# Attention in groups of three token tiles behind accumulating gathers, and gate sums fetched by DMA

## The chip, the cores and the metric

One core of a Trainium2 chip runs the whole kernel as one program. The metric is device time in microseconds (us). Three runs of the kernel before took 1563.63, 1563.95 and 1555.30 us, median 1563.63.

## The reference, cut to what matters

```
h = tok(x)                                    # patches of 16 frames, layer norm, matmul, layer norm
h = h + power_attention(layernorm(h))         # 8 heads x 2 queries, gates
h = h + experts(layernorm(h))                 # top 4 of 16 experts, and a shared one
h = h + rope_softmax_attention(layernorm(h))  # 16 heads, 4 key heads
h = h + bitlinear_ffn(layernorm(h))

# power attention, per head
logG = cumsum(log_sigmoid(6.906768 + x @ Wg))
a = (q k^T / sqrt(d))**2 * exp(logG[t] - logG[s]), causal;  y = (a @ v) / sum(a)

# experts
acc + cw[:, None] * (silu(x @ wg.T) * (x @ wu.T)) @ wd.T      # cw is 0 outside a token's top 4
```

There are 64 sequences of 23 tokens, so T = 1472 tokens, in NT = 12 tiles of 128 rows. All sums are f32; a product is split in two f16 halves and made as three matmuls (`split3`, L852 to L854).

## The kernel before

Five instruction streams (SP for most transfers, POOL for indirect and other transfers and small arithmetic, ACT, PE, DVE) run side by side and meet at semaphores. There is no scheduler: the order on every engine is the order in the text.

**First attention.** A loop over 8 heads and, in it, over 4 chunks c of 16 sequences (CW = 368 tokens, as four blocks of AT = 92). For each chunk PE projects q, q and k (`head_project`, 12 matmuls each), then v (48 matmuls), makes the squared scores' products (L950), the output projection of the chunk before (`out_proj`), the weighted sum (L967), and turns the result (L983). The gate exponent logG[t] - logG[s] needs, in each of 92 partitions, the sum of one head's gates along the row. Before, that row is made anew for each chunk: DVE multiplies the log gates by a triangle (L1447, tile `Dg`), PE multiplies by a matrix of ones (L935), ACT copies it from PSUM (L635, tile `gt`), and DVE subtracts logG and adds the mask (L1450, L1452). At the end of a head ACT and DVE split the next head's weights in halves (`unit_a_hi` L550, `unit_a_lo` L1295), and in chunks 1 and 3 one expert's weights (`expert_hi` L627, `expert_lo` L1295).

Ahead of the first head, PE computes the gate logits (`gate_logits`), DVE and ACT their log sigmoid, and PE sums it (L904) before it projects anything.

**Experts.** A token's rows go to expert tiles of 128 slots; results are kept in DRAM (`yslot`, L480). The shared expert's tiles 6 to 11 come last. Then 48 indirect transfers (12 tiles x 4, `collect`, L484) fetch each token's four results to a scratch tile, three tiles deep, and DVE adds them up and into the row h (`returned`, L1698 to L1701). Statistics of the rows (`total_stats`, L1313), a root on POOL (L446) and shifts (L1327) follow for tiles 0 to 7 and then for 8 to 11.

**Second attention.** ACT normalizes 12 tiles (L560), PE turns them (L847), ACT and DVE split them (L565, L1332). Then the chunks c = 0 to 3 of 368 tokens: PE makes six projections (`project`: j = 0 to 3 q, 4 k, 5 v, the last at L1161), ACT moves them (`moved`, L743, L738), DVE shuffles (L1743), POOL multiplies by cosine and sine (`cosine`, L516, L517), DVE adds (`rotated`, L1753, L1754), PE makes 16 x 4 small score products (`scores`, L1177), DVE masks and centres (L1761, L1764, L1765), ACT exponentiates (L747), DVE divides (`weights`, L1771, L1772, L1777), PE turns (`turn`, L1186) and multiplies by V (`weighted`, L1199), and ACT and DVE split the result (L760, L1784). The output projection (`out_rows`), the last norm and the feed-forward layer follow.

PE's order there is scores(c), project(c + 1, 0 to 5), turn(c), weighted(c), scores(c + 1). All 12 tiles are turned before scores(0).

## Time and profile before

| | |
|---|---|
| median of three runs | 1563.63 us |
| profiled execution | 1547.85 us, span 1545.9 us |
| mean granted TensorE clock | 0.915 |
| busy: PE, DVE, ACT, POOL | 1316.9, 937.2, 644.0, 283.0 us |
| start to 143 us | tokens and first norms |
| 143 to about 707 us | first attention, 8 heads |
| about 707 to 1124 us | routing and experts |
| 1124 to 1190 us | 48 gathers |
| 1190 to 1341 us | second attention |
| 1341 us to the end | output projection, feed-forward |

Times in the rows are counted from the span's start. A busy time that is larger than the distance to the next start means pipelined work: for matmuls the distance between starts is what one costs. "idle before <- X" names what the engine waited for. The clock is a share of the full 2.4 GHz, so 0.50 is 1.2 GHz.

### The profile page before, as it was taken

How to read it: one execution, taken by the hardware profiler on the slowest of the kernel's cores; microseconds unless marked ns; L12 is line 12 of the kernel's file. 1: busy time of each engine (PE TensorE's matmuls, PEld its weight loads, DVE VectorE, ACT ScalarE, POOL GpSimd, SP SyncE). 2: the span in 40 equal slices, each digit the busy share in tenths (PEclk: the TensorE clock that was granted, in tenths of full speed). 3: DMA queues.
4: the chain of work that ended last, by engine and by line, in shares of the span. 5: the costliest groups of instructions: out<-in, count | busy, mean ns of one | idle time of the engine just before them, and what ended most of it. 6: DMA issues, size and time to landing. Idle time of an engine off the chain costs nothing.

```text
span 1545.9 us, 30851 instructions
## 1 busy us (share of the span) xinstructions
PE 1316.9 (85%) x10735; PEld 837.6 (54%) x10736; DVE 937.2 (61%) x1940; ACT 644.0 (42%) x1098; POOL 283.0 (18%) x342
## 2 busy tenths in 40 slices
PE   6887999999999999996759999999950788668997
PEld 3445767677776777774424444444520566424443
DVE  5775456556665555658663555554376455588886
ACT  3445434444444444542314444444420433126664
POOL 2443000000000000000012233233276334020000
PEclk9986999999999999996779999999985778689999
DMA  5222142423334342421315767874265000000000
GB/s 177 69 102 69 56 170 116 163 109 135 133 132 170 136 163 82 163 83 75 132 62 181 258 240 256 283 241 162 91 193 168 2 2 3 1 1 8 21 20 31
DMA packets 40254, 179.87 MB, mean 116 GB/s; under 512 B 8512, under 2 KB 9024, under 8 KB 32384
## 3 DMA queue, kind: packets, MB, share of 16 engines
q0 software_dynamic: 18208, 95.41, 17.4%
q1 hardware_dynamic: 18528, 71.03, 13.0%
q10 hardware_dynamic: 3456, 12.58, 2.4%
q8 instruction: 41, 0.67, 0.2%
q14 instruction: 21, 0.17, 0.0%
HBM read 131.32 MB, written 47.69 MB: 116 GB/s over the span
## 4 chain that ended last, share of the span: by engine, by line
PE 56%; DVE 18%; issue 13%; POOL 6%; ACT 5%; DVEq 1%; DMA 1%; ACTq 0%; POOLq 0%; SPq 0%
PE ps L852 14%; PE ps L853 13%; PE ps L854 13%; POOL wide L484 3%; PE ps L967 3%; PE ps L950 3%; PE ps L1177 2%; DVE ff L1870 2%; DVE amf L1877 1%; PE ps L935 1%; PE ps L983 1%; DVE wa_lo L1295 1%; POOL rt_out L446 1%; PE ps L1046 1%; PE ps L1248 1%
## 5 line engine op out<-in xcount | busy, mean ns | idle before, releaser
L852 PE MATMUL ps<-nT_hi,wa_hi 128*128 128x368 f16 x448 | 146.4, 327 | 15.9 <-DVE wa_lo L1295 15.9
L853 PE MATMUL ps<-nT_lo,wa_hi 128*128 128x368 f16 x448 | 146.0, 326 | 0.0
L854 PE MATMUL ps<-nT_hi,wa_lo 128*128 128x368 f16 x448 | 145.6, 325 | 0.0
L476 POOL DMA_INDIRECT xg<-xrow,idx x61 | 61.1, 1001 | 277.1 <-PE ps L1046 101.7
L1629 DVE SCALAR_TENSOR_TENSOR nrm<-ps,xg,nrm 128x256 f32<-128x256 f32 x61 | 29.5, 484 | 133.5 <-ACT nrm L694 107.6
L852 PE MATMUL ps<-wa_hi,nT_hi 128*92 128x128 f16 (+1 forms) x560 | 108.8, 238 | 0.0
L853 PE MATMUL ps<-wa_lo,nT_hi 128*92 128x128 f16 (+1 forms) x560 | 107.6, 236 | 0.0
L854 PE MATMUL ps<-wa_hi,nT_lo 128*92 128x128 f16 (+1 forms) x560 | 107.6, 236 | 0.0
L852 PE MATMUL ps<-wide,xT 128*128 x244 | 93.4, 383 | 12.3 <-issue 6.3
L663 ACT ACTIVATE yT_hi<-ps 128x368 f16<-128x368 f32 x64 | 27.2, 474 | 164.0 <-PE ps L983 164.0
L471 POOL DMA_DIRECT2D wsp<-we_sp x16 | 8.6, 537 | 468.7 <-DVE we_sp L1295 468.7
L1432 DVE SCALAR_TENSOR_TENSOR wide<-ps,wide 128x368 f32<-128x368 f32 x128 | 69.1, 540 | 41.0 <-PE ps L854 41.0
L853 PE MATMUL ps<-wide,xT 128*128 x244 | 93.2, 382 | 0.0
L854 PE MATMUL ps<-wide,xT 128*128 x244 | 93.0, 381 | 0.0
L1248 PE MATMUL ps<-qw,qT 128*128 128x512 bf16 x384 | 89.1, 387 | 2.7 <-DVE ff L1870 2.6
L852 PE MATMUL ps<-yT_hi,wb_hi 128*128 128x368 f16 x256 | 82.6, 323 | 1.2 <-DVE yT_lo L1479 1.2
L853 PE MATMUL ps<-yT_lo,wb_hi 128*128 128x368 f16 x256 | 82.6, 323 | 0.0
L854 PE MATMUL ps<-yT_hi,wb_lo 128*128 128x368 f16 x256 | 82.6, 323 | 0.0
L622 ACT ACTIVATE qk<-ps 128x368 f32<-128x368 f32 x96 | 45.2, 478 | 89.1 <-PE ps L854 89.0
L1457 DVE TENSOR_TENSOR a<-sq,E 92x368 f32<-92x368 f32 x64 | 31.7, 534 | 82.3 <-ACT sq L651 82.3
L852 PEld LDWEIGHTS ps<-wa_hi,nT_hi 128*92 128x92 f16 (+1 forms) x560 | 67.4, 120 | 22.3 <-ACT qk L622 17.2
L685 ACT ACTIVATE xT<-ps 128x1024 f16<-128x1024 f16 x61 | 62.3, 1024 | 28.9 <-PE ps L1046 21.2
(307 smaller groups left out, 3403.9 us busy)
## 6 DMA issues: line engine op xcount, KB each, us to landing
we_st<-in_we POOLq DMA_DIRECT2D x16, 1536.0 KB, 6.9
wsp<-we_sp POOLq DMA_DIRECT2D x16, 1536.0 KB, 5.4
wide<-wsp SPq DMA_DIRECT2D x16, 1536.0 KB, 7.4
yslot<-yt POOLq DMA_DIRECT2D x61, 256.0 KB, 4.3
wq_st<-in_ffq SPq DMA_DIRECT2D x24, 512.0 KB, 4.5
wq_st<-in_ffq ACTq DMA_DIRECT2D x24, 512.0 KB, 3.9
wide<-in_wa SPq DMA_DIRECT2D x10, 1024.0 KB, 4.8
xt<-in_x SPq DMA_DIRECT2D x12, 512.0 KB, 3.5
```

The source lines that it names most:

```text
L476: pool.indirect_dma_start(Q["xg"][:, g % 4, :].bitcast(U32), None, xrow, bass.IndirectOffsetOnAxis(ap=idx[:, g:g + 1], axis=0)).then_inc(x ...
L484: pool.indirect_dma_start(h1[:, 4 * (k % 3) + j, :], None, yslot, bass.IndirectOffsetOnAxis(ap=slot[:, k, j:j + 1], axis=0)).then_inc(xg_i ...
L622: nc.scalar.activation(B["qk"][:, j, :], ps[:, (5 * c + j) % 2, 0:CW], ACT.Copy, scale=1.0 / WS).then_inc(b_ev, 1)
L685: nc.scalar.activation(Q["xT"][:, p].rearrange("p a b -> p (a b)"), ps[:, p, :].bitcast(F16), ACT.Copy).then_inc(m_xe, 1)
L852: nc.tensor.matmul(dst, lhs[0], rhs[0], start=start, stop=False)
L853: nc.tensor.matmul(dst, lhs[0], rhs[1], start=False, stop=False)
L854: return nc.tensor.matmul(dst, lhs[1], rhs[0], start=False, stop=stop)
L950: ins = nc.tensor.matmul(ps[0:AT, 2 + j, a * REP * AT:(a + 1) * REP * AT], B["qk"][:, 2, tok], B["qk"][:, 0:2, tok], start=True, stop=True)
L967: ins = nc.tensor.matmul(ps[0:AT, 4 + 2 * j + a, r * (DH + 1):(r + 1) * (DH + 1)], B["a"][0:AT, j, a, r, :], B["v1"][0:AT, 2 * j + a, :], ...
L1248: ins = nc.tensor.matmul(ps[:, 2 * (f % 2) + q, :], Gm["qT"][:, b, ds(k * P, P)], qw[:, q, b * FF + f * 512:b * FF + (f + 1) * 512], start ...
L1432: V.scalar_tensor_tensor(acc, ps[:, 6 + blk % 2, 0:CW], 1.0 / (WS * AS), acc, ALU.mult, ALU.add).then_inc(b_acc, 1)
L1457: V.tensor_tensor(B["a"][0:AT, j], B["sq"][0:AT, j], B["E"][0:AT, 2 * j:2 * j + 2].unsqueeze(2).broadcast_to([AT, 2, REP, AT]), ALU.mult). ...
```

## The change

(1) The gate sums are made once. PE forms them for all heads with the heads on partitions (a second small matmul beside L904's), DVE copies them (`lgt`), SP writes them to DRAM (`lgd`) and, for each head, fetches the row of one head broadcast to 92 partitions (`gr`, 92 x 1472 f32, 541.7 KB). L1447, L935 and L635 go. The first two projections now stand ahead of the gate sums on PE. At the end of a head the next head's weights are split ahead of the expert's.

(2) The 48 gathers add into the rows h themselves (`compute_op=ALU.add`). The four of one tile run one behind the other: each waits for the one before. DVE's four additions of a tile go. Those of tiles 0 to 5 are issued in rounds of six; those of tiles 6 to 11 in rounds of three, between POOL's other work.

(3) Statistics, roots, normalization and turning of the rows run in groups of three tiles, two groups ahead of or between the chunks of the second attention, which on PE now runs as project(c, 2 to 5), turn(c - 1), scores(c), weighted(c - 1), with the first two projections of a chunk ahead of it. DVE makes the sine products of chunk 0 and of j = 4. Scores wait for the copy out of PSUM (`f_cp`), no longer for the split result of the chunk just before.

```diff
-        h1 = flat.rearrange("p (k d) -> p k d", d=D)
...
+        lgd = nc.dram_tensor("lgd", (HEADS, T), F32, kind="Internal").ap()
...
+sp.wait_ge(g_lg, 2)
+sp.dma_start(lgd.rearrange("h (a p) -> (h a) p", p=AT), B["lgt"][:, :]).then_inc(init_out, 16)
+sp.wait_ge(init_out, 32)
+sp.dma_start(B["gr"][0:AT], lgd[0:1, :].broadcast_to([AT, T])).then_inc(gr_in, 16)
+with sp.Fori(0, HEADS - 1) as i:
...
     unit_b(i + 1)
+    sp.wait_ge(b_gr, i + 1)
+    sp.dma_start(B["gr"][0:AT], lgd[ds(i + 1, 1), :].broadcast_to([AT, T])).then_inc(gr_in, 16)
...
-def collect(k):
-    for j in range(TOPK):
-        pool.indirect_dma_start(h1[:, 4 * (k % 3) + j, :], None, yslot,
-                                bass.IndirectOffsetOnAxis(ap=slot[:, k, j:j + 1], axis=0)).then_inc(xg_in[k % 3], 16)
...
+def share(k, j):
+    if j or k >= 6:
+        pool.wait_ge(sh_in[k % 6], SHARES[k % 6] + 64 * (k // 6) + 16 * j)
+    pool.indirect_dma_start(h[:, k, :], None, yslot, bass.IndirectOffsetOnAxis(ap=slot[:, k, j:j + 1], axis=0),
+                            compute_op=ALU.add).then_inc(sh_in[k % 6], 16)
+def shares(g, j):
+    for k in range(GT * g, GT * g + GT):
+        share(k, j)
...
-for k in range(NT):
-    if k >= 3:
-        pool.wait_ge(c_h, ready(NT + k - 3))
-    collect(k)
...
-for n, x in enumerate((slice(0, EARLY), slice(EARLY, NT))):
-    root(rc_ask, 2 + n, rt_in[:, x], rt_out[:, x], rc_done)
...
+def turned_root(g):
+    x = slice(GT * g, GT * g + GT)
+    root(rc_ask, 2 + g, rt_in[:, x], rt_out[:, x], rc_done)
...
-    nc.gpsimd.tensor_tensor(Fm["qs"][:, j, :], Fm["qs"][:, j, :], sinT[:], ALU.mult).then_inc(f_cos, 1)
...
+    if c and j < 4:
+        nc.gpsimd.tensor_tensor(Fm["qs"][:, j, :], Fm["qs"][:, j, :], sinT[:], ALU.mult).then_inc(f_cos, 1)
...
+for j in range(TOPK):
+    shares(0, j)
+    shares(1, j)
+pool.wait_ge(m_y, VT)
+shares(2, 0)
+turned_root(0)
+nc.gpsimd.memset(Fm["qp"][:, :, :, SL:], 0.0).then_inc(f_pad, 1)
+shares(3, 0)
+turned_root(1)
+cosine(0, 0)
+shares(2, 1)
+cosine(0, 1)
+cosine(0, 2)
+shares(2, 2)
+cosine(0, 3)
+cosine(0, 4)
+shares(2, 3)
+pool.wait_ge(wa_lo, UNITS + 1)
+nc.gpsimd.memset(st_a[:], 0.0).then_inc(f_pad, 1)
+shares(3, 1)
+for j in range(5):
+    cosine(1, j)
+shares(3, 2)
+turned_root(2)
+shares(3, 3)
+turned_root(3)
+for c in range(2, CH):
     for j in range(5):
         cosine(c, j)
-    if c == 0:
-        nc.gpsimd.memset(Fm["qp"][:, :, :, SL:], 0.0).then_inc(f_pad, 1)
-        pool.wait_ge(wa_lo, UNITS + 1)
-        nc.gpsimd.memset(st_a[:], 0.0).then_inc(f_pad, 1)
...
-        act.wait_ge(b_pj, 5 * g + 4)
-        nc.scalar.activation(B["gt"][0:AT].rearrange("p a b -> p (a b)"),
-                             ps[0:AT, (5 * c + 3) % 2, 0:CW], ACT.Copy).then_inc(b_ev, 1)
...
+        if c == CH - 1:
+            unit_a_hi(i + 1, b_pj, 4 * CH * (i + 1))
         if c in (1, 3):
             expert_hi(2 * i + c // 2)
-        if c == CH - 1:
-            unit_a_hi(i + 1, b_pj, 5 * CH * (i + 1))
...
+def normed(k):
+    if k % GT == 0:
+        act.wait_ge(ln_sh, 3 + k // GT)
+    ln_norm(2, k, k % 2)
...
+normed(0)
+normed(1)
+high(0)
+normed(2)
+high(1)
+high(2)
+moved(0, 0)
+moved(0, 1)
 for c in range(CH):
-    if c + 1 < CH:
-        for j in range(2):
-            moved(c + 1, j)
-    exponential(c)
-    if c + 1 < CH:
-        for j in range(2, 6):
-            moved(c + 1, j)
-    weights_turned(c)
-    y_high(c)
+    k = GT * (c + 1)
+    if c % 2 == 0:
+        normed(k)
+        normed(k + 1)
+    moved(c, 2)
+    if c % 2 == 0:
+        high(k)
+        normed(k + 2)
+    moved(c, 3)
+    if c % 2 == 0:
+        high(k + 1)
+    moved(c, 4)
+    if c % 2 == 0:
+        high(k + 2)
+    moved(c, 5)
+    if c == 0:
+        act.wait_ge(wa_in, 16 * (UNITS + 1))
+        nc.scalar.activation(wo[0][:].rearrange("p a b -> p (a b)"), st_a[:], ACT.Copy, scale=WS).then_inc(wa_hi, 1)
+    else:
+        weights_turned(c - 1)
+    if c == 1:
+        normed(k)
+        normed(k + 1)
+        exponential(c)
+        y_high(c - 1)
+        high(k)
+        normed(k + 2)
+        high(k + 1)
+        high(k + 2)
+        moved(c + 1, 0)
+        moved(c + 1, 1)
+    else:
+        if c + 1 < CH:
+            moved(c + 1, 0)
+            moved(c + 1, 1)
+        exponential(c)
+        if c:
+            y_high(c - 1)
+weights_turned(CH - 1)
+y_high(CH - 1)
 def f_square(k, p, half):
...
-pe.wait_ge(g_lg, 1)
-nc.tensor.matmul(ps[0:AT, 7, 0:16 * HEADS], tri[0:AT, :], B["lg"][0:AT].rearrange("p a b -> p (a b)"),
-                 start=True, stop=True).then_inc(g_cum, 1)
...
-        pe.wait_ge(b_ev, free(5 * g + 3))
-        pe.wait_ge(b_D, g + 1)
-        nc.tensor.matmul(ps[0:AT, (5 * c + 3) % 2, 0:CW], ones[0:AT, 0:AT], B["Dg"][0:AT].rearrange("p a b -> p (a b)"),
-                         start=True, stop=True).then_inc(b_pj, 1)
-        pe.wait_ge(b_ev, free(5 * g + 4))
+        pe.wait_ge(b_ev, free(4 * g + 3))
...
 for j in range(2):
     head_project(0, 0, j)
+pe.wait_ge(g_lg, 1)
+nc.tensor.matmul(ps[0:AT, 7, 0:16 * HEADS], tri[0:AT, :], B["lg"][0:AT].rearrange("p a b -> p (a b)"),
+                 start=True, stop=True)
+nc.tensor.matmul(ps[:, 6, 0:AT], B["lg"][0:AT].rearrange("p a b -> p (a b)"), tri[0:AT, :],
+                 start=True, stop=True).then_inc(g_cum, 1)
 with pe.Fori(0, HEADS - 1) as i:
     head(i, False)
 head(HEADS - 1, True)
...
+    if j == 0:
+        pe.wait_ge(ln_lo, ready(2 * NT + GT * c + GT - 1))
...
-    if c:
-        pe.wait_ge(f_lo, 4 * c)
+    if c == 1:
+        pe.wait_ge(f_cp, 1)
+    if c > 1:
+        pe.wait_ge(f_lo, 4 * (c - 1))
...
     pe.wait_ge(f_s, c + 1)
+    pe.wait_ge(ln_lo, ready(2 * NT + min(NT, GT * (c + (3 if c % 2 else 2))) - 1))
...
     pe.wait_ge(f_ev, 6 * c + 7)
+    if c + 1 < CH:
+        pe.wait_ge(f_cp, c + 2)
+    else:
+        pe.wait_ge(f_lo, 4 * c)
...
-for k in range(NT):
-    ln_turn(2 * NT + k, k % 2, 2 + k % 4, 2 * NT + k - 1)
-    if k == 6:
-        pe.wait_ge(wa_lo, UNITS)
-    if k in (6, 8, 10):
...
+def row_turn_l1(k):
...
+for k in range(GT):
+    row_turn_l1(k)
+pe.wait_ge(wa_lo, UNITS)
...
+project(0, 0)
+project(0, 1)
 for c in range(CH):
+    k = GT * (c + 1)
+    for j in range(2, 6):
+        project(c, j)
+        if c % 2 == 0 and j < 5:
+            row_turn_l1(k + j - 2)
+    if c:
+        turn(c - 1)
+    if c == 0:
+        project(c + 1, 0)
+        project(c + 1, 1)
     scores(c)
-    if c + 1 < CH:
-        for j in range(6):
-            project(c + 1, j)
-    turn(c)
-    weighted(c)
+    if c == 1:
+        weighted(c - 1)
+        for j in range(GT):
+            row_turn_l1(k + j)
+    if 0 < c < CH - 1:
+        project(c + 1, 0)
+        project(c + 1, 1)
+    if c > 1:
+        weighted(c - 1)
+turn(CH - 1)
+weighted(CH - 1)
...
     pe.wait_ge(w_h, free(k))
+    pe.wait_ge(f_lo, 4 * ((min(T, P * k + P) - 1) // CW) + 4)
...
 dve.wait_ge(g_cum, 1)
+V.tensor_copy(B["lgt"][:], ps[:, 6, 0:AT]).then_inc(g_lg, 1)
...
-        V.tensor_tensor(B["Dg"][0:AT], B["lgh"][0:AT, 4 * c:4 * c + 4].unsqueeze(2).broadcast_to([AT, 4, AT]),
-                        tri[0:AT].unsqueeze(1).broadcast_to([AT, 4, AT]), ALU.mult).then_inc(b_D, 1)
-        dve.wait_ge(b_ev, ready(5 * g + 3))
-        order(V.tensor_tensor(B["gt"][0:AT], B["gt"][0:AT],
+        if c == 0:
+            dve.wait_ge(gr_in, 16 * (i + 1))
+            dve.sem_inc(passed, 1)
+        order(V.tensor_tensor(B["gt"][0:AT], B["gr"][0:AT, c * CW:(c + 1) * CW].rearrange("p (a t) -> p a t", a=4),
                               B["LGh"][0:AT, 4 * c:4 * c + 4].unsqueeze(2).broadcast_to([AT, 4, AT]), ALU.subtract))
+        if c == CH - 1:
+            dve.sem_inc(b_gr, 1)
         V.tensor_tensor(B["gt"][0:AT], B["gt"][0:AT], mask[0:AT].unsqueeze(1).broadcast_to([AT, 4, AT]),
...
+        if c == CH - 1:
+            unit_a_lo(i + 1)
         if c % 2:
             expert_lo(2 * i + c // 2, 0)
-        if c == CH - 1:
-            unit_a_lo(i + 1)
...
-def returned(k):
-    dve.wait_ge(xg_in[k % 3], SLOTS_IN[k % 3] + 64 * (k // 3 + 1))
-    dve.sem_inc(passed, 1)
-    y = [h1[:, 4 * (k % 3) + j, :] for j in range(TOPK)]
-    V.tensor_tensor(y[0], y[0], y[1], ALU.add)
-    order(V.tensor_tensor(y[2], y[2], y[3], ALU.add))
-    order(V.tensor_tensor(row(k), row(k), y[0], ALU.add))
-    V.tensor_tensor(row(k), row(k), y[2], ALU.add).then_inc(c_h, 1)
...
-    dve.wait_ge(c_h, ready(NT + k))
+    dve.wait_ge(sh_in[k % 6], SHARES[k % 6] + 64 * (k // 6 + 1))
...
+def group_stats(g):
+    for k in range(GT * g, GT * g + GT):
+        total_stats(k)
+    deviations(2, GT * g, GT * g + GT, rc_ask)
...
+def group_shift(g):
+    shifts(2 + g, GT * g, GT * g + GT, rc_done)
...
+group_stats(0)
+group_shift(0)
+group_stats(1)
...
+    if c == 0 or j == 4:
+        dve.wait_ge(f_sh, 5 * c + j + 1)
+        dve.sem_inc(passed, 1)
+        V.tensor_tensor(Fm["qs"][:, j, :], Fm["qs"][:, j, :], sinT[:], ALU.mult).then_inc(f_cos, 1)
...
     dve.wait_ge(f_sc, c + 1)
...
+    V.tensor_tensor(S.rearrange("p (g h) s -> p g h s", g=G4),
+                    ps[:, 2:6, 0:CW].rearrange("p g (h s) -> p g h s", s=SL),
+                    mask1[:].unsqueeze(1).unsqueeze(1).broadcast_to([P, G4, 16, SL]), ALU.add).then_inc(f_cp, 1)
+    dve.wait_ge(f_cp, c + 1)
...
+for k in range(GT):
+    low(k)
+group_shift(1)
 for c in range(CH):
+    k = GT * (c + 1)
+    rotate(c, 0)
+    rotate(c, 1)
+    if c:
+        weights(c - 1)
+    for j in range(2, 5):
+        if c % 2 == 0:
+            low(k + j - 2)
+        rotate(c, j)
+    rotated(c)
+    if c == 0:
+        dve.wait_ge(wa_hi, UNITS + 1)
+        split_lo(wo[1][:].rearrange("p a b -> p (a b)"), st_a[:], wo[0][:].rearrange("p a b -> p (a b)"), wa_lo)
+    if c == 1:
+        group_stats(2)
+        group_shift(2)
     centred(c)
-    if c + 1 < CH:
-        for j in range(2):
-            rotate(c + 1, j)
-    weights(c)
-    if c + 1 < CH:
-        for j in range(2, 5):
-            rotate(c + 1, j)
-        rotated(c + 1)
-    y_low(c)
+    if c:
+        y_low(c - 1)
+    if c == 1:
+        for j in range(GT):
+            low(k + j)
+        group_stats(3)
+        group_shift(3)
+weights(CH - 1)
+y_low(CH - 1)
```

## Rows read from the trace of the kernel before

**Rows 1.** Windows: us, busy of PE, PEld, DVE, ACT, POOL (instructions), PE clock, DMA share, GB/s
```profile
283.40:351.80 68.40, 66.09 (x568) 49.76 (x568) 40.55 (x80) 30.00 (x51) 2.15 (x4) 1.00 0.37 138
...
1124.30:1190.30 66.00, 18.48 (x99) 8.57 (x97) 46.17 (x80) 9.18 (x16) 51.62 (x49) 0.68 0.69 201
1190.30:1229.00 38.70, 22.51 (x304) 16.21 (x304) 20.40 (x39) 19.50 (x31) 14.36 (x14) 0.72 0.03 11
1229.00:1259.60 30.60, 25.53 (x528) 19.25 (x528) 15.46 (x22) 9.36 (x16) 9.33 (x10) 0.78 0.01 3
...
1317.20:1340.60 23.40, 12.65 (x273) 11.54 (x274) 9.00 (x6) 3.82 (x5) 0.00 (x0) 0.53 0.01 1
```

**Rows 2.** Timeline of PE, end of a head and next chunk: start, busy, line, shape, idle before
```profile
285.68 0.33 PE L852 MATMUL ps<-nT_hi,wa_hi 128*128 128x368 f16 x1 [2.28 <-DVE wa_lo L1295]
...
287.56 0.80 PE L983 MATMUL ps<-ident,yn 92*128 92x92 f32 x8
288.19 0.32 PE L852 MATMUL ps<-nT_hi,wa_hi 128*128 128x368 f16 x1
...
295.67 0.79 PE L935 MATMUL ps<-Dg,ones 92*92 92x368 f32 x2
296.40 0.26 PE L852 MATMUL ps<-wa_hi,nT_hi 128*92 128x128 f16 x1
```

**Rows 3.** Timeline of DVE at the same head boundary
```profile
283.26 2.29 DVE L1295 SCALAR_TENSOR_TENSOR wa_lo<-wide,wa_hi 128x2048 f16<-128x2048 f32 x1
...
286.85 0.69 DVE L1473 TENSOR_TENSOR yn<-ps,rn 92x512 f32<-92x512 f32 x1
```

**Rows 4.** Timeline of PE at the start of the first attention
```profile
151.30 0.73 PE L904 MATMUL ps<-lg,tri 92*92 92x128 f32 x2 [6.13 <-DVE lg L1418]
...
165.52 0.72 PE L967 MATMUL ps<-v,a 92*92 92x129 f32 x5
```

**Rows 5.** DMA issues: tile, queue, kind, count, KB each, median us to landing
```profile
xt<-in_x SPq DMA_DIRECT2D x12, 512.0 KB, 3.5
...
tb<-in_tb SPq DMA_DIRECT2D x1, 256.0 KB, 9.2
...
xrow<-cwt SPq DMA_DIRECT2D x1, 96.0 KB, 2.6
```

**Rows 6.** The gathers, L484: durations on POOL in ns, and to landing
```profile
L484 POOL DMA_INDIRECT wide<-yslot,slot x48: 942/948/2623, 1124.3 to 1189.2; - x48
...
DMA to landing us min/median/max: 3.3/3.7/7.3
```

**Rows 7.** Timeline of PE in the second attention
```profile
1197.39 1.97 PE L847 MATMUL ps<-ident,nrm 128*128 128x128 f32 x8 [52.36 <-ACT nrm L560]
...
1228.94 7.04 PE L1177 MATMUL ps<-kr,qp 32*128 32x23 f32 x128 [6.87 <-DVE qp L1754]
1235.91 0.49 PE L852 MATMUL ps<-nT_hi,wa_hi 128*128 128x368 f16 x1
1239.57 0.51 PE L852 MATMUL ps<-nT_hi,wa_hi 128*128 128x368 f16 x1
1241.80 0.32 PE L852 MATMUL ps<-nT_hi,wa_hi 128*128 128x368 f16 x1
1243.67 0.32 PE L852 MATMUL ps<-nT_hi,wa_hi 128*128 128x368 f16 x1
```

**Rows 8.** Timelines of DVE, ACT and POOL in the second attention
```profile
1236.05 1.69 DVE L1761 TENSOR_TENSOR wide<-ps,mask 128x1472 f32<-128x1472 f32 x1 [7.16 <-PE ps L1177]
...
1247.56 1.69 DVE L1777 TENSOR_TENSOR wide<-wide,rd 128x1472 f32<-128x1472 f32 x1
...
1243.79 1.43 ACT L747 ACTIVATE wide<-wide 128x1472 f32<-128x1472 f32 x1
...
1241.76 0.97 POOL L516 TENSOR_TENSOR qraw<-qraw,cosT 128x368 f32<-128x368 f32 x1 [13.06 <-DVE qs L1743]
```

**Rows 9.** Timeline of PE, last chunk of the second attention
```profile
1334.97 3.83 PE L1186 MATMUL ps<-ident,wide 128*128 128x128 f32 x16 [10.74 <-DVE wide L1777]
```

More of the change, by code:

```diff
@@ L390, in _ @@
                 unit_b(i + 1)
+                sp.wait_ge(b_gr, i + 1)
+                sp.dma_start(B["gr"][0:AT], lgd[ds(i + 1, 1), :].broadcast_to([AT, T])).then_inc(gr_in, 16)
+            sp.wait_ge(q_abs, 3 * HEADS - 2)
+            for m in range(3):
+                sp.dma_start(wq_st[:, m, :], t["ffq"][m, HEADS - 1]).then_inc(q_in, 16)
+            sp.wait_ge(wa_lo, HEADS)
+            unit_a(HEADS)
+            sp.wait_ge(wb_lo, HEADS)
+            unit_b(HEADS)
             for k in range(NT):
@@ L760, in y_high @@
                     nc.scalar.activation(cols, ps[:, 2 + j, 0:CW].rearrange("p (w a t) -> p a w t", w=4, a=J4), ACT.Copy).then_inc(f_hi, 1)
-            for k in range(NT + 1):
-                if k in (0, EARLY):
-                    act.wait_ge(ln_sh, 3 + k // EARLY)
-                if k < NT:
-                    ln_norm(2, k, k % 2)
-                if k:
-                    ln_high(2 * NT + k - 1, k - 1, 2 + (k - 1) % 4)
-                if k in (8, 10, 12):
-                    moved(0, (k - 8) // 2)
@@ L918, in head_project @@
             def head_project(g, c, j):
-                pe.wait_ge(b_ev, free(5 * g + j))
+                pe.wait_ge(b_ev, free(4 * g + j))
                 cols = slice(c * CW, (c + 1) * CW)
                 for b in range(KD):
-                    ins = split3(ps[:, (5 * c + j) % 2, 0:CW], [wa[x][:, b, j * P:(j + 1) * P] for x in range(2)],
+                    ins = split3(ps[:, j % 2, 0:CW], [wa[x][:, b, j * P:(j + 1) * P] for x in range(2)],
                                  [nT[x][:, b, cols] for x in range(2)], b == 0, b == KD - 1)
@@ L940, in head @@
                         for b in range(KD):
-                            ins = split3(ps[0:AT, (5 * c + 4) % 2, a * P:(a + 1) * P], [nT[x][:, b, tok] for x in range(2)],
+                            ins = split3(ps[0:AT, 1, a * P:(a + 1) * P], [nT[x][:, b, tok] for x in range(2)],
                                          [wa[x][:, b, 3 * P:4 * P] for x in range(2)], b == 0, b == KD - 1)
                     ins.then_inc(b_pj, 1)
-                    pe.wait_ge(b_ev, ready(5 * g + 2))
+                    pe.wait_ge(b_ev, ready(4 * g + 2))
                     for j in range(2):
@@ L959, in head @@
                         out_proj(g - 1, c - 1)
[L960 removed]
+                    pe.wait_ge(b_ev, ready(4 * g + 3))
                     for j in range(2):
@@ L1236, in q_turn @@
                 ins.then_inc(w_tr, 1)
-            pipeline(pe, NT, [(0, out_rows)])
+            for k in range(NT):
+                out_rows(k, k % 2, k // 2)
             def gate_up(k, fs):
```

79 lines of the change are left out of this document (25 added, 54 removed).

## The prediction, made before the kernel was run

> **What bounds the kernel now.** I read the page's engine table and slices first: PE is busy 1316.9 of 1545.9 us, but the slices show two places where it is not, around 1150 us and from there to 1345 us. Then the windows. In the first attention PE works 66.1 of 68.4 us of a head at full clock [rows 1]: what comes off PE there comes off the time. From 1124.3 to 1190.3 PE works 18.5 of 66 us, all of it ahead of 1145; POOL issues 48 gathers, 51.6 us busy, and nothing after them can start. From 1190.3 to 1229 PE works 22.5 of 38.7, and then 25.5 of 30.6 in the first chunk and 12.7 of 23.4 in the last [rows 1]. So PE is idle 87 us between 1124.3 and 1340.6: 216.3 less the busy 128.9 (the six windows; the two chunks not shown are like the one that is). The chain of waits says the same: POOL L484 one behind the other, then DVE, ACT, PE in turn. This is what the change goes at.
>
> **Part 1, gate sums.** Each of 32 chunks loses the ones matmul: from its start at 295.67 to the next group's at 296.40 is 0.73 us of PE [rows 2]. A first weight load after it stays, so I take 0.70: 32 x 0.70 = **22.4 us**. Ends: 0.62, if more of the load stays, and 0.73, so 20 to 23.4. Nothing takes its place: v's projection waits for bank 1, which ACT empties while q or k is still projected; scores wait for k's copy, which runs under 2.7 us of v. DVE (40.6 of 68.4 busy) and ACT lose 0.5 us each per chunk, off the path, so nothing.
>
> The row of the next head is asked for when chunk 3's subtraction has run, some 24 us ahead of its use. The longest broadcast here took 9.2 us for 256 KB among many others, 512 KB in plain form 3.5 us [rows 5]; for 541.7 KB either is hidden after head 0. If that cover failed it would cost the excess once a head.
>
> At the start, PE was idle 6.13 us for the gates and came to the first weighted sum at 165.52 [rows 4]. Now two projections fill that. At 1.2 GHz a projection costs 3.66 us (1235.91 to 1239.57), at full clock 1.87 (1241.80 to 1243.67) [rows 7]; after such thin work the clock rose about 4 us into dense work, so both take some 6 us: 145.5 to 151.4, just as the gates are done. Gate sums 0.6, k's projection 1.9, v 2.7, scores 1.3, next projection 1.9: PE is at the weighted sum at 159.8. The row arrives by another way: sums 152.0, copy 0.4, write 2.6 [rows 5], broadcast 3.5 to 9.2, then two DVE operations, the exponential and the product, 2.3: 160.8 to 166.5. Against 165.52, less the 0.7 counted above: +4.0 to -1.7; I take **3.5**, near the transfer of twice the size.
>
> At a head's end PE waits 2.28 us for the next weights [rows 2]. They now come 1.15 us earlier (one expert operation less ahead). But the next step, the turns at 287.56, needs yn, which DVE ends at 287.54 as before [rows 3]. So of 1.15 only the projection's tail is gained, 0.2 x 7 = **1.4 us** (ends 0 and 8).
>
> Part 1: **27.3 us**, ends 18 and 35.
>
> **Parts 2 and 3, gathers and pipeline.** Now 48 gathers take 66 us, 1.37 each: 0.95 on POOL and 0.30 between, some longer [rows 6]. Only tiles 0 to 5 are needed for the first two groups: 24 gathers. No row shows an accumulating gather. Below, it can't beat a plain one: same indices, same rows. Above: POOL's longest single one took 2.6, landing 3.7 median [rows 6]. I take the plain pace at its undisturbed value, 1.30, since DVE's adds no longer run beside it; the nearest row is this one. Rounds of six then are 7.8 us apart, more than the 3.7 of a landing, so the wait for the tile's gather before costs nothing.
>
> The walk, all from the rows: 24 gathers 1124.3 to 1155.5. shares(2, 0) three more: 1159.4. Stats of tiles 0 to 2 are done at 1158; root 1160.3, shift, normalize, turn, split of three tiles 6.2 (an estimate: 0.8 to normalize, two turns in 2.0 [rows 7], a third, and two splits of 0.6 each): 1166.7. Projections (0, 0), (0, 1) 5.6, three with turns between 6.9, v about 4, (1, 0) and (1, 1) 3.7: 1187.4. POOL beside it: shares(3, 0), root, one product, shares(2, 1), two, shares(2, 2), two: 1184.5, and DVE's addition ends at 1186.7. So scores(0) starts at **1187.4, was 1228.94** [rows 7]: 41.5 earlier.
>
> Then chunk by chunk. scores 7.0 to 1194.4; centring 3 x 1.7 and the exponential with its table 2.7 end at 1202.2 [rows 8]. In ACT's queue `moved(1, 2)` stands behind that exponential, so PE waits about 4.6 us before project(1, 4), and v ends at 1208.7; weights(0) is ready by then (4.0 us). turn(0) 2.3; scores(1) waits for POOL, whose ten products of 0.97 are queued behind shares(3, 1): 1213.6 to 1220.7. weighted(0) to 1224.2. The three turns of tiles 6 to 8 wait for ACT, which has exponential(1) and the copy of y(0) ahead: PE is idle till 1233. What is late is that, not the gathers: shares(2, 3) landed at 1192 and shares(3, 3) at about 1225. Projections (2, 0) to (2, 5) with turns 17, turn(1) 2: scores(2) 1252 to 1259; (3, 0), (3, 1), weighted(1), (3, 2) to (3, 5): 1274.3; turn(2) to 1276.5; scores(3) waits for the shuffles and products of chunk 3, which stand behind weights(2) on DVE: 1282.2 to 1289.3. The last chunk's tail stays as it was: centring, exponential, weights (and y_low(2), 1.8, now ahead of them), turn and weighted 5.6 with idle 10.74 before [rows 9]: the second attention ends at **1306, was 1340.6** [rows 1]. That is 34.5. The walk has some twenty handoffs between engines and I counted most as free; I take 4.5 off: **30 us**.
>
> PE idle by this walk is about 54 of 182 us, against 87 of 216, with the same 129 us of work: all the gain is idle time.
>
> DVE's 12 x 4 additions are counted at nothing: they ran under POOL's issue. Its extra sine products (8 of 0.54) lie under POOL's queue; uncovered 4.3 us. The order of out_rows changes nothing. The clock: it is 0.50 in scores and for 4 us after [rows 7], as before, once a chunk.
>
> **Sum.** 27.3 + 30 = 57.3 us. 1547.85 - 57.3 = 1490.5 for an execution like the profiled one. That lies 15.8 below the median of the runs, 1563.63, so the median forecast is **1506 us**.
>
> **A rule against it.** The shares of the gathers' windows are 0.69 at one gather per 1.37 us [rows 1]: the 16 queues need 0.95 us for a plain one. If an accumulating gather needs twice the queues' time, 1.9 us, it is paced by them and not by POOL: 24 x (1.9 - 1.3) = 14 us later, of which the second half's slack gives some 4 back. The Trainium skill (Collectives: The Full Stack, section "The bandwidth ceiling") says that an add in the transfer's path needs two source reads for each write, and so runs at half the rate of a copy; by it the sum is 1516.
>
> **Rivals.**
> (a) The gather paced at 1.9 us by the queues, as just worked out: B is 20 instead of 30, 1516 us. For it: the share of 0.69 leaves no room for a doubling. Against it: no row has such a transfer. Chance 0.27.
> (b) The new order trades one wait for another: the walk's waits at ACT (4.6 and 8.8 us) and at POOL grow, since cosines of chunk 1 stand behind gathers that may not have landed (3.7, at most 7.3 [rows 6]). Four chunks with 4 us more each: 1522 us. Chance 0.15.
> (c) Slower than before: accumulating gathers do not overlap on the queues, so each costs a whole landing, 3.7 us [rows 6]. The first 24 take 89 instead of 31: 57 us later, and tiles 9 to 11 would still be short of theirs when group 3 is due, some 15 more: 1506 + 72 = 1578. It decides from about 3.1 us a gather. Against it: plain gathers overlap three deep. Chance 0.05.
> (d) The gate row is late in every head, or PE's 0.7 turns into another wait: part 1 gives 5, 1528. For v and scores the rows show no such wait. Chance 0.04.
> My own case: chance 0.49.
>
> **Numbers.** Own case alone 1492 to 1518. The range takes in (a), (b) and (d) and an execution level 8 us below the median: **1486 to 1534**. About 1% (15.6 us) can be told from no change: faster by over that, under 1548, is my case with (a), (b), (d) less their tails, **0.90**; same **0.05**; slower **0.05**, case (c) and worse.
>
> **What would show it.** In the profile after: no L935-like matmul, and a head of 65.5 instead of 68.4 us; the distance of first to 24th gather near 31 us (44 speaks for (a), 89 for (c)), with the DMA share of that window near 0.7 or above 0.9; scores(0) about 63 us after the first gather (was 104.6), and the output projection 182 after it (was 216.3). PE's wait for ACT in chunk 1 and ahead of tiles 6 to 8. I am wrong if the heads are not shorter, or if POOL's time for one gather has changed.

## The result, and the profile after

The changed kernel takes **1511.47 us** (median of four runs, 1510.59 to 1511.60) against 1560.72 for the kernel before in the same comparison: ratio 0.969, 95% interval 0.965 to 0.972. The forecast was 1506, the range 1486 to 1534. Profile against profile it is 1511.43 against 1547.85, 36.4 us; the forecast had 57.3. So the median came near the forecast by luck, through two errors that cancel: 21 us too much gain, and a distance of 15.8 us between profile and runs that the changed kernel does not have.

Windows of the profile after (columns as in [rows 1]): one head of the first attention; a stretch with nothing but gathers; from the first projection to scores(0); and from scores(2)'s end to scores(3).

```profile
195.60:261.00 65.40, 63.83 (x564) 49.08 (x563) 38.22 (x74) 28.51 (x49) 2.16 (x4) 1.00 0.42 154
1125.00:1150.00 25.00, 0.00 (x0) 0.00 (x0) 5.25 (x5) 0.38 (x1) 21.31 (x13) 0.58 0.95 170
1157.60:1186.80 29.20, 22.75 (x304) 15.11 (x304) 16.11 (x32) 12.35 (x20) 22.38 (x17) 0.85 0.60 92
1252.90:1280.80 27.90, 23.38 (x525) 17.14 (x525) 15.96 (x23) 8.47 (x17) 10.09 (x9) 0.88 0.01 3
```

A head takes 65.16 us now (the distance at which SP asks for the gate rows), where it was 68.40 [rows 1]: 3.2 less; the forecast had 65.5. In the second window PE stands still and the DMA share is 0.95. Beside plain gathers, in a window of the kernel before with PE standing still too, it was 0.73:

```profile
1156.00:1188.00 32.00, 0.00 (x0) 0.00 (x0) 20.71 (x40) 0.00 (x0) 24.69 (x25) 0.50 0.73 214
```

The start of the first head, from the timeline (start, duration, engine, line, idle before and what ended it):

```profile
152.33 0.36 PE L1065 MATMUL ps<-tri,lg 92*128 92x92 f32 x2
154.71 0.28 SPq L393 DMA_DIRECT2D gr<-lgd  x1
163.86 0.54 DVE L1550 TENSOR_TENSOR gt<-gr,LGh 92x368 f32<-92x368 f32 x1 [10.01 <-DMA gr<-lgd]
166.59 3.72 PE L1036 MATMUL ps<-v,a 92*92 92x129 f32 x16 [5.31 <-DVE a L1559]
```

The gate row (`gr`) took 9 us from its request to DVE's first use, and PE comes to its weighted sum at 166.59, later than before's 165.52 [rows 4] and not earlier. PE had stood idle for 5.3 us, and behind that its clock is at half:

```profile
166.30:173.10 6.80, 6.50 (x26) 4.99 (x27) 3.86 (x9) 1.25 (x2) 0.00 (x0) 0.50 0.34 124
```

The gathers (duration in ns: min/median/max), to be laid beside [rows 6], and then PE's longest waits from there to the output projection, whose first matmul is the last row:

```profile
L506 POOL DMA_INDIRECT h<-yslot,slot x48: 1537/1547/3534, 1104.4 to 1221.9; - x48
```
```profile
1158.36 1.97 PE L924 MATMUL ps<-ident,nrm 128*128 128x128 f32 x8 [34.14 <-ACT nrm L606]
...
1186.75 6.96 PE L1255 MATMUL ps<-kr,qp 32*128 32x23 f32 x128 [2.66 <-DVE qp L1845]
1200.89 0.33 PE L929 MATMUL ps<-nT_hi,wb_hi 128*128 128x368 f16 x1 [1.64 <-ACT qraw L786]
...
1213.50 2.77 PE L1255 MATMUL ps<-kr,qp 32*128 32x23 f32 x48 [5.21 <-DVE qp L1845]
...
1230.35 1.09 PE L924 MATMUL ps<-ident,nrm 128*128 128x128 f32 x4 [3.73 <-DVE nT_lo L1432]
...
1280.80 3.44 PE L1255 MATMUL ps<-kr,qp 32*128 32x23 f32 x88 [3.15 <-DVE qp L1845]
...
1299.39 3.75 PE L1265 MATMUL ps<-ident,wide 128*128 128x128 f32 x16 [8.85 <-DVE wide L1870]
1304.67 0.39 PE L929 MATMUL ps<-wo_hi,nT_hi 128*128 128x512 f16 x1
```

A gather holds POOL for 1.55 us, not 0.95; with the 0.30 between that is 1.85. The table gives each event of this stage in us behind the first gather. root(g) is POOL's square root for the norms of group g (three tiles), scores(c) PE's first score product of chunk c; "end" is the first matmul of the output projection:

| | before | forecast | after |
|---|---|---|---|
| first gather, from the span's start | 1124.3 | 1097 | 1104.4 |
| 24 gathers issued | 33.0 | 31.2 | 46.4 |
| root(0), of the first norms | 65.9 | 35.1 | 51.4 |
| scores(0) | 104.6 | 63.1 | 82.4 |
| second attention ends | 216.2 | 181.7 to 186 | 200.3 |

(The forecast's own walk ended at 181.7; with the 4.5 it took off the gain, 186.) Part 1 is the difference in the first row: 20.0 us. Parts 2 and 3 are the difference in the last: 15.9.

### The profile page after: what moved, and what is told of

Its sections match the earlier page's. It is cut to its first block, busy times and chain, and to the rows that moved or that the text cites. A ratio compares the mean times of both kernels' runs of the same rounds, so it can differ in the third digit from the quotient of the medians.

```text
span 1509.5 us, 30358 instructions
## 1 busy us (share of the span) xinstructions
PE 1294.1 (86%) x10660; PEld 829.6 (55%) x10674; DVE 896.4 (59%) x1865; ACT 629.5 (42%) x1066; POOL 308.6 (20%) x336
## 4 chain that ended last, share of the span: by engine, by line
PE 55%; DVE 18%; issue 13%; POOL 7%; ACT 4%; DMA 2%; DVEq 1%; ACTq 0%; POOLq 0%; SPq 0%
PE ps L929 14%; PE ps L931 13%; PE ps L930 13%; POOL h L506 3%; PE ps L1036 3%; PE ps L1019 3%; PE ps L1255 2%; DVE ff L1976 2%; DVE amf L1983 1%; PE ps L1120 1%; PE ps L1052 1%; POOL rt_out L466 1%; PE ps L1348 1%; PE ps L1366 1%; POOL qraw L539 1%
## 5 line engine op out<-in xcount | busy, mean ns | idle before, releaser
L506 POOL DMA_INDIRECT h<-yslot,slot x48 | 80.8, 1684 | 15.4 <-issue 13.1
```

The source lines that it names most:

```text
L506: pool.indirect_dma_start(h[:, k, :], None, yslot, bass.IndirectOffsetOnAxis(ap=slot[:, k, j:j + 1], axis=0), compute_op=ALU.add).then_inc ...
```

## Experiments

Each kernel is one edit of the kernel before or of the changed one. "The first profile" is the one of [rows 1 to 9].

### Do the two halves add up?

Gate only is the kernel before with the part of the change from `lgd` to the order of the splits; groups only is the changed kernel with that part taken back. The core of the edit:

```diff
-                    nc.tensor.matmul(ps[0:AT, (5 * c + 3) % 2, 0:CW], ones[0:AT, 0:AT], B["Dg"]...
+            sp.dma_start(B["gr"][0:AT], lgd[0:1, :].broadcast_to([AT, T])).then_inc(gr_in, 16)
```

> The kernel before with part 1 alone (gate sums by the DMA broadcast; gathers, their additions and the second attention as before). My theory: the changed kernel's trace has its first gather 20.0 us earlier than before's (1104.36 instead of 1124.34), so part 1 is worth 20 us: a profiled execution 20 us under before's 1547.85, near 1528, and by the timed runs of the same call a median 20 us under before's. Rival 1 (the two parts lean on each other, the groups profit from an earlier start of transfers): part 1 alone gives 10 or less. Rival 2, on the distance between runs and profile: before's runs lie 13 to 16 us above its profiled execution and the changed kernel's don't; if what takes that distance away is part 1, the timed gain here is 33 or more while the profiles show 20; if it is parts 2 and 3, the distance stays and both show 20.

> The changed kernel with part 1 taken back (gate sums by the ones matmul again; gathers that add, and the pipeline over groups, stay). My theory: the profiles show 16 us less than before's (near 1532), the timed runs about 16 less too if part 1 took the distance between runs and profile away, or 29 if parts 2 and 3 did. 24 gathers take 46 us, 1.85 each, scores of the first chunk start 82 us after the first gather, the end of the second attention is 200 us after it, as in the changed kernel. Rival (the parts lean on each other): the sum of this gain and of the other part's alone differs from 49 by over 8 us.

Measured: gate only 1539.42 against 1555.45 for before (ratio 0.990, 0.987 to 0.993), 16.0 us, its profile 1539.92 where I expected 1528; groups only 1533.98 (0.985, 0.983 to 0.988), 21.5 us. The sum is 37.5. I had set 49 against it, the gain of the first comparison, and 8 us of difference as the sign that the parts lean on each other: it differs by 11.5. But 49 had a before of 1560.72 in it. Against this comparison's 1555.45 the changed kernel's 1511.47 is 44.0 less, and the sum is 6.5 short.

The traces say where. I compare with the second profile of before, taken in the next section, whose time (1555.38) is that of these runs. Gate only has its first gather at 1103.24, 21.6 us earlier, but its second stage takes 228.5 us where before, with the same code there, takes 223.2: 5.3 us lost. Groups only has 24 gathers at 1.85 us, scores(0) at +82.6 and the end at +201.9, nearly as in the changed kernel (+82.4, +200.3), and 21.3 less than 223.2. So each part does its own work, and what is missing is mostly those 5.3 us, for which I have no cause.

Groups only shows one thing more. Four of its runs lie at 1533 to 1535 and two at 1541.5; the profiled one is of the latter. One of its heads:

```profile
283.40:351.80 68.40, 66.12 (x560) 49.65 (x559) 39.82 (x78) 28.58 (x51) 2.15 (x4) 0.98 0.35 133
```

The granted clock (third number from the end) is 0.98, where [rows 1] has 1.00: it falls to half (1.2 GHz) for a moment in five of the eight heads, each time just behind a head's end, where PE has waited 2.28 us for the next weights. The first gather comes 7.9 us later than in the first profile, 1.6 for each fall. The same wait of 2.28 us is in both profiles of before, without a fall.

### Why the kernel before runs above its profile

> The kernel before, unchanged, to see a second profile of it. My theory: time near 1555, and its profile has four or more falls of the granted clock to half for 3.4 us in the heads (between 175 and 690 us), where the first profile (1547.85) had none; each is worth 1.7 us. Rival: the profile is near 1555 without such falls, and the 8 us lie in the gathers' stage (1124 to 1229 us), by a stall of PE and ACT near the experts' end as in the gate-only kernel.

> The kernel before with one edit of part 1 alone: the split of the next head's weights goes ahead of one expert's split on ACT and DVE. PE's wait at the end of each head (2.28 us) shrinks by about 1.15. My theory of the distance between runs and profile: in most runs of the kernel before the granted clock falls to half for 3.4 us at that wait, once in most heads, 1.7 us each (the groups-only kernel's profile has five such falls and is 8 us above its other runs, the profile of before has none). With the shorter wait the falls go, as they are gone in the changed kernel: this kernel is timed near its own profile, at 1547 or a little under, 7 to 12 us under before's runs. Rival 1: it is the ones matmul or another part of part 1 that made them go: the time is within 3 us of before's runs. Rival 2: the distance is of the gathers' stage: the same, and no falls in either profile.

```diff
 (ACT; DVE's expert_lo and unit_a_lo likewise)
-                    if c in (1, 3):
-                        expert_hi(2 * i + c // 2)
                     if c == CH - 1:
                         unit_a_hi(i + 1, b_pj, 5 * CH * (i + 1))
+                    if c in (1, 3):
+                        expert_hi(2 * i + c // 2)
```

Before again is the kernel before once more: profile 1555.38, no falls of the clock in the heads, first gather at 1124.84, but the end of the second attention at +223.2 instead of +216.2. So the rival holds for this execution: the 8 us are in the gathers' stage. ACT's waits between 1124 and 1150 us, of this profile and then of the first (total, times, longest):

```profile
ACT hT L689 <- remote: 11.5, 1, 11.5
ACT hT L689 <- PE ps L1063: 3.0, 2, 1.5
```
```profile
ACT hT L689 <- PE ps L1063: 6.7, 5, 1.5
```

While the experts' last tiles run beside the gathers, ACT once starts 11.5 us late ("late ACT" from here on); PE and DVE stand behind it, DVE's additions of the gathered rows stand behind them, and POOL then waits 8.1 us for a scratch tile. The first profile has none of this.

Weights first: 1555.51 against 1558.19 (0.997, 0.995 to 0.999), where I expected 7 to 12 us less. PE's wait at a head's end fell from 2.28 [rows 2] to 1.14 us; the profile, 1552.91, has no falls in the heads and the late ACT (8.0 and 4.3 us). Of its 12 runs none lies above 1558.4, where 10 of 23 runs of before in that comparison lie between 1563 and 1567, all with a mean clock of 0.905 to 0.909, and the other 13 with 0.912 to 0.919.

So my theory was wrong in its number (1547) and half right in its cause. The best account that I have is that the kernel before has **two costs that come and go**: about 7 us of late ACT beside the gathers, and about 8 us of clock at the heads' ends. Its profile of 1547.85 had neither and that of 1555.38 the first; in the last comparison below, on another chip, its median was 1548.26. The first cost is seen in a profile of before. The second is inferred: no profile of before with falls was taken, and that they are its 1563 rests on groups only's profile and on the mean clocks of the runs. That part 1's earlier weights take the second away rests on the 12 runs of weights first; how often the first occurs, two profiles can't tell. The comparisons ran on several chips, and no experiment separates the chip from these costs.

### What an adding gather costs

> The changed kernel with the additions left out of the gathers: each gather overwrites the row, so the output leaves out the residual and three of four experts' results. My theory: the addition in the transfer is what cost 15 of the 19 us that the first scores were later than forecast; here a gather takes 1.25 to 1.37 us instead of 1.85, 24 of them 31 us instead of 46, scores of the first chunk start 63 to 68 us after the first gather instead of 82.4, DMA share of the first 24 near 0.7 instead of 0.95, and the time is 12 to 18 us under the changed kernel's, near 1496. Rival 1: it is the order of the gathers or their target in the token rows, not the addition: a gather still takes 1.8. Rival 2: the gathers are faster but the pipeline behind them gives it back at the waits on ACT and POOL: 24 in 31 us, and the time within 5 us of 1511.

> The changed kernel with every adding gather on the first 256 of 512 columns: the additions to the other columns are left out. Half the bytes, the same count of rows. My theory: GpSimd is busy 1.55 us with issuing an adding gather, and 1.55 + 0.30 between is the 1.85 seen, so half the bytes change nothing: 1.75 to 1.85 us a gather, DMA share falls from 0.95 to about half, time within 5 us of 1511. Rival (the queues pace: 1.76 us of all 16 for an adding gather of 256 KB, and GpSimd's 1.55 holds back-pressure from them): a gather falls to 1.25 to 1.3, 24 in 31 us, time 12 to 18 us less.

> The plain-write kernel (additions left out, as there), with a small memset ahead of 18 of its first 24 gathers, so that they are some 1.7 to 1.9 us apart as adding ones are, not 1.26. In the plain-write kernel ACT twice started over 11 us late while the experts' last tiles ran beside the gathers, and the experts ended 43 us after the first gather instead of 20. Theory 1 (it is the pace of the plain gathers): no wait of ACT over 3 us there, the experts end at +20 to +24, root(0) at +40 to +47. Theory 2 (it is their kind, 4 KB packets instead of 2 KB, whatever the pace): ACT's waits of 8 to 12 us stay, the experts end at +35 or later.

```diff
 plain write                                    half row
-        ..., compute_op=ALU.add)               -  pool.indirect_dma_start(h[:, k, :], ...
+        ...)                                   +  pool.indirect_dma_start(h[:, k, 0:D // 2], ...
 plain paced (on plain write), first 18 gathers
+    nc.gpsimd.memset(flat[:, 0:448], 0.0).then_inc(f_pad, 1)
+    pool.wait_ge(f_pad, 6 * j + k + 1)
```

The gathers' rows, of plain write, half row and plain paced:

```profile
L506 POOL DMA_INDIRECT h<-yslot,slot x48: 946/953/2755, 1101.8 to 1212.3; - x48
```
```profile
L506 POOL DMA_INDIRECT h<-yslot,slot x48: 1538/1547/3535, 1106.4 to 1222.7; - x48
```
```profile
L509 POOL DMA_INDIRECT h<-yslot,slot x48: 946/954/2188, 1102.4 to 1208.2; - x48
```

The addition costs POOL 0.60 us a gather, whatever the bytes: half row has 1.547 too, and it is timed 1510.83, the same as 1511. Its DMA share beside the gathers is 0.65 instead of 0.95, not the half that I expected:

```profile
1130.00:1150.00 20.00, 0.00 (x0) 0.00 (x0) 2.09 (x4) 0.00 (x0) 16.65 (x12) 0.50 0.65 119
```

So **POOL's issue paces the adding gather, not the queues** (theory of half row, its rival out). The queue lines of the profile's page show what else grew; before, after, plain write:

```profile
q0 software_dynamic: 18208, 95.41, 17.4%
```
```profile
q0 software_dynamic: 21280, 95.41, 20.3%
```
```profile
q0 software_dynamic: 18208, 95.41, 17.8%
```

The same bytes in 3072 packets more, 64 for each of 48 gathers: by the trace's packets a plain gather is 64 of 4 KB, an adding one 128 of 2 KB. Whether POOL's 0.60 us are for the 64 packets more or for the addition as such, no run separates: the half-row kernel has 128 packets a gather too, of 1 KB.

Plain write does 24 gathers in 30 us, as expected, and still gains little: 1506.33 where I expected 1496, scores(0) at +80.0 where I expected 63 to 68. The late ACT is back. Its timeline:

```profile
1110.59 0.42 ACT L738 ACTIVATE hh<-nrm 128x256 f16<-128x256 f32 x1 [0.49 <-DVE nrm L1730]
1122.51 0.60 ACT L731 ACTIVATE hT<-ps 128x512 f16<-128x512 f16 x1 [11.50 <-remote]
1134.44 0.38 ACT L736 ACTIVATE nrm<-ps 128x256 f32<-128x256 f32 x1 [11.33 <-remote]
```

PE's transposes that `hT` reads are recorded at 1111.6, yet ACT starts at 1122.5, and again 11.3 us late. The experts end at +43 instead of +20.6, and POOL waits 13.3 us for them. In plain paced the first 18 gathers are 1.71 us apart, the last six 1.26 as before. It has no such wait; its three largest (total, times, longest):

```profile
ACT hT L734 <- PE ps L1139: 7.1, 5, 1.5
ACT nrm L739 <- PE ps L933: 2.8, 4, 0.7
ACT hh L741 <- DVE nrm L1733: 2.5, 5, 0.5
```

With its gathers slower, its second stage is **7.9 us shorter**: root(0) at +43.0, scores(0) at +74.3, the end at +189.5 instead of +197.4. In time that is 1498.8 in the profiled run and 1504.9 in the only other one, against 1505.85 to 1513.46 for plain write: too few to tell a size. This speaks for theory 1, the pace. The late ACT is in four profiles with gathers 1.26 us apart (before again, gate only, weights first, plain write: 8.0 to 11.5 us), not in the fifth, the first profile, and in none of the eight with adding ones. But only one profile has plain gathers at the slower pace, and since one of five escapes at the fast pace too, that it is the pace and not the kind is likely, not shown. How either reaches a signal from PE to ACT, no trace shows; the profile's name for the releaser is only "remote", and no packet of the queues that carry instructions (q8, q14) moves during these waits.

### The gate row's broadcast

> The changed kernel with the gate row broadcast to 96 partitions instead of 92; the four more are never read. My theory: the row of the first head is late because its broadcast takes about 9 us (asked for at 154.7, DVE has it at 163.9 after a wait of 10.0), and it does so because 92 rows are dealt to few of the 16 DMA engines; 96 divides by 16. Then the broadcast takes 3 to 5 us, DVE's wait falls to 4 to 6, PE's first weighted sum comes 4 to 5 us earlier and the time is 1507. Rival: the time is that of 12 KB rows written to so many partitions, whatever their number, or of the other transfers of that moment: the wait stays near 10 and the time at 1511.

```diff
-            sp.dma_start(B["gr"][0:AT], lgd[0:1, :].broadcast_to([AT, T])).then_inc(gr_in, 16)
+            sp.dma_start(B["gr"][0:96], lgd[0:1, :].broadcast_to([96, T])).then_inc(gr_in, 16)
```

```profile
158.57 0.54 DVE L1550 TENSOR_TENSOR gt<-gr,LGh 92x368 f32<-92x368 f32 x1 [4.97 <-DMA gr<-lgd]
```
```profile
161.30 1.97 PE L1036 MATMUL ps<-v,a 92*92 92x129 f32 x16 [0.26 <-DVE a L1559]
```

4% more bytes, and the wait halves: 10.01 to 4.97. In the trace the 92 packets of the row (5888 B each) take 7.1 us, with 4.0 of them under way at a time on average; the 96 take 2.4 us, with 13.2 under way. The Trainium skill (DMA: Bandwidth & Descriptors, section "Why a DMA increments its semaphore by 16 and not by 1") says that a transfer is dealt to the largest number of engines up to 16 that divides the slowest dimension of both its sides; it names 16 for 96 partitions, and for 92 the rule gives 4. The traces agree with it.

The time is 1501.58 (0.963, 0.961 to 0.966), 9.9 under the changed kernel, twice what I expected. The trace accounts for 9.0 of it by the first gather (1095.33): 5.3 at this wait, and 3.2 more by the next turns on PE. The same 16 matmuls take 1.97 us instead of 3.72: behind PE's idle 5.3 us the changed kernel's clock is at half from 166.3 to 173.1, and here it stays full.

### The order of the gathers

> The changed kernel with the gathers of a group of three tiles in sequence (12 for tiles 0 to 2 first, then 3 to 5) instead of two groups in turn, the first group's root behind 18 gathers instead of 27, and group 1's norms behind all six projections of chunk 0. An adding gather waits for the one before it on the same row; three tiles at 1.85 us are 5.55 us, the landing seen is 5.5. My theory: GpSimd's 1.85 us a gather sets the start of the second attention, so root(0) comes 33 to 36 us after the first gather instead of 51.4, scores of the first chunk 63 to 68 instead of 82.4, the end of the second attention 182 to 187 instead of 200.3; time 1493 to 1498. Rival 1: an adding gather cannot start until the one before on its rows has landed in full, 5.5 us plus issue, so rounds of three take 7 us or more: 12 gathers in 28 us, and under half of the gain, 1504. Rival 2: GpSimd's queue is the bound of the whole stage, not of its start: scores of the first chunk are early, the end of the second attention stays within 4 us of 200.

> The group-by-group order and the 96-partition row together. The two touch different stages, so the gains should add: 1511.5 - 5.9 - 9.9 = 1495.7, between 1493 and 1499. Rival: the row's gain was of one chip's state (the wait fell by 5, the time by 9.9): 1500.

> As both, and three moves around chunks 0 and 1: PE does the scores of chunk 0 ahead of group 1's turns and the first two projections of chunk 1, GpSimd does chunk 1's cosines ahead of the last group's gathers, and DVE takes the four sine products of chunk 1. My theory: in the group-by-group kernel scores of chunk 0 waited for group 1's last landing (root of group 1 at +62.4, scores at +76.3), and scores of chunk 1 for cosines that stood behind gathers. Here scores(0) come at +66 to +70, scores(1) at +95 to +98, the end of the second attention at +188 to +192 (was +195.5), time 1489 to 1493. Rival: GpSimd's 48 gathers set the time of group 2's root (+106) whatever the order around them: the end stays at +194 to +196, time 1495.

> The kernel of both, with the 1 MB load of the output weights held back until group 1's root is done (it was asked for 22 to 24 us after the first gather, beside the gathers), and its split on ACT behind the first two moves of chunk 1. My theory: that load took the queues from the adding gathers: GpSimd then waited 4.4 us for a landing ahead of group 1's second round. Without it that wait is under 1.5 us, root(0) comes at 34 to 36 us instead of 38.9, scores of chunk 0 at 72 to 74 instead of 77.3, the end of the second attention at 189 to 191 instead of 194.0; time 1491 to 1492. Rival 1: the wait is the adding gathers' own backlog and stays: 1495.5. Rival 2: the load, later, meets the gathers of groups 1 and 2, and the 4 us are lost there: root(0) earlier, the end within 1 us of 194.

"Both" is group by group together with the row to 96; the last two kernels are edits of both.

```diff
 group by group (POOL; ACT, PE and DVE do chunk 0's projections ahead of group 1's norms)
             for j in range(TOPK):
                 shares(0, j)
-                shares(1, j)
+            shares(1, 0)
+            shares(1, 1)
+            turned_root(0)
...
 scores first (on both; and GpSimd's cosines of chunk 1 ahead of shares(3, 0))
+                scores(c)
                 if c == 0:
                     for j in range(GT):
                         row_turn_l1(k + j)
                     project(c + 1, 0)
                     project(c + 1, 1)
-                scores(c)
...
 late load (on both)
             sp.wait_ge(wa_lo, UNITS)
+            sp.wait_ge(rc_done, 4)
             sp.dma_start(st_a[:], t["wo"]).then_inc(wa_in, 16)
```

| | time (median) | root(0) | scores(0), (1), (2), (3) | end |
|---|---|---|---|---|
| changed kernel | 1511.47 | 51.4 | 82.4, 109.1, 148.5, 176.4 | 200.3 |
| group by group | 1505.59 | 38.6 | 76.3, 103.6, 143.7, 171.7 | 195.5 |
| both (with the row to 96) | 1495.55 | 38.9 | 77.3, 103.0, 142.2, 170.1 | 194.0 |
| scores first | 1499.78 | 39.1 | 64.4, 101.7, 145.6, 172.0 | 195.8 |
| late load | 1493.98 | 35.2 | 71.8, 99.5, 139.0, 167.0 | 192.9 |

I had expected 1493 to 1498 of group by group, with root(0) at 33 to 36 and the end at 182 to 187. Root(0) comes 12.8 us earlier by the order, and 4.8 are left at the end, close to rival 2, which had at most 4. Its rival 1 is out: 12 gathers take 23 us, not 28. The gains of both add as expected (1495.7). Scores first shows most clearly that an early start is not enough: scores(0) 13 us earlier than in both, the end no earlier, the median 4 us worse, though the runs overlap; I had expected 1489 to 1493. Where root(0) of group by group was later than I worked out, the wait has an address. POOL, and SP:

```profile
1131.56 1.55 POOL L506 DMA_INDIRECT h<-yslot,slot  x1 [0.30 <-issue]
1137.21 1.55 POOL L506 DMA_INDIRECT h<-yslot,slot  x1 [4.10 <-DMA h<-yslot,slot]
```
```profile
1126.16 0.33 SPq L441 DMA_DIRECT2D wide<-in_wo  x1
```

The 1 MB of the output weights, asked for at 1126, met the gathers of 1128. With that load later (last kernel, where ACT's split of it moves back too) POOL's longest wait of that stretch is 0.7 instead of 4.4, and root(0) is 3.7 us earlier; 1.1 of it reaches the end, nearly its rival 2. All versions place root(2), which the second pair of chunks needs, at +102 to +112, and in all five scores(2) follows it by 35 to 37 us. Until root(2) POOL issues 42 gathers (45 in the changed kernel), 78 us by themselves at 1.85, and the cosines and roots that stand between them. So POOL's queue ahead of root(2) is what the end hangs on; this is read from the traces, no run takes gathers out of that queue.

Both and late load beat both kernels: 0.961 (0.958 to 0.964) and 0.963 (0.961 to 0.966) of the kernel before, the latter against a before of 1548.26. Their difference, 1.6 us from two comparisons, is not told apart.

## Why the prediction was right, and where it was not

**Gate sums, 22.4 us.** Right, a little small: from one weighted sum (L967, after L1036) to the next within a head the changed kernel is 0.71 to 0.78 us shorter, so the whole 0.73 of the matmul comes off, the upper end of the term, 23.4.

**Start, 3.5 us.** This step failed, in sign: the first weighted sum is 1.1 us later instead of 3.5 plus 0.7 earlier, so -1.8 in the sum's terms, a hair past its lower end of -1.7. The bound of 9.2 us for the broadcast, from the longest row, was the true value; I took 3.5, the row of a plain transfer of 512 KB. The experiment with 96 partitions shows that the count of partitions, not the bytes, set it: there the weighted sum comes at 161.30, 4.2 us earlier than before's, which is the 3.5 plus 0.7. And the wait cost what the sum had nowhere: the clock falls behind it, and the second weighted sum comes another 2.5 us later where it should come 0.7 earlier, 3.2 in all. So the start gave -5.0.

**Head ends, 1.4 us.** Right: across a head's end the distance between weighted sums shrinks by 0.98 to 1.00, 0.25 more than inside a head, 1.8 for seven ends. The earlier weights probably also end the falls of the clock, which the first profile could not show.

Part 1 in all: 23.4 - 5.0 + 1.8 = 20.2, and 20.0 was measured where I had 27.3. The miss is the start alone.

**Parts 2 and 3, 30 us: 15.9.** Here the step that failed is "I take the plain pace": 1.85 us a gather, not 1.30. I had named as a sign that I am wrong "if POOL's time for one gather has changed", and it has, from 0.95 to 1.55 us. That put the 24th gather 15.2 us later. Scores(0) came 19.3 later; 3 of the other 4 are in the stretch from root(0) to scores(0), 31.0 us where the walk had 28. Rival (a) had the size (1.9 us, 1516) and the wrong mechanism: the packets did double, and the share of the queues rose to 0.95, but the half-row kernel shows that POOL's issue is the slower of the two. The Trainium skill (Collectives: The Full Stack, section "The bandwidth ceiling") has half the rate for transfers that add, measured on a ReduceScatter between cores. The queues' time here is near it (0.95 of 1.85 is 1.76 us an adding gather, against 0.69 of 1.37, 0.95, a plain one) and does not set the pace. From scores(0) on the walk had 118.6 us and 117.9 were measured, with PE's wait for the turns of tiles 6 to 8 at 3.7 where I had 8.8, for ACT in chunk 1 at 1.6 where I had 4.6, and a wait of 5.2 for POOL's products in chunk 1 where I had 2.6; so the 4.5 us taken off for handoffs were not needed. Rival (b) is out.

**"That lies 15.8 below the median."** I carried the distance over unchanged, and the changed kernel has none: its four runs lie within 1.0 us of each other, its profile among them. By the account above, the distance is made of two costs of the kernel before that this change happens to remove, since its gathers add at a slower pace and its weights come earlier. Nothing in the prediction foresaw that. Against the second profile of before (1555.38) the change brings 43.9: 20.5 up to the first gather, 22.9 in the second stage.

**Rivals (c) and (d).** Gathers overlap (24 in 46.4, not 89), and the row is late only once.

Open: what delays ACT beside plain gathers; how much the pace of the gathers by itself is worth, since no run has the walk's 1.30 us without the late ACT; why gate only's second stage is 5 us longer than before again's (4.3 of it lie behind scores(0), away from the late ACT); and whether all of before's 1563 us are falls of the clock.

## What to carry to other kernels

Price a transfer from a row with the same count of partitions and the same kind, not only the same bytes: an addition doubled a gather's packets and cost its issuing engine 0.60 us, and 92 partitions instead of 96 cost 5 us of waiting and, through the clock, 3 more. When runs lie above the profile, ask for a second profile before carrying the distance over: it may be a stall that the change removes. And where one engine issues everything that a pipeline waits for, bringing the first result forward can give most of it back later: here 12.8 us at root(0) were 4.8 at the end.
